# Macaron transformer block on 8 cores: four in-flight copy and square tiles instead of two in the layer-norm statistics of the attention stage

## What is computed

```python
def _layernorm(x, axis=-1, eps=1e-5):
    m = jnp.mean(x, axis=axis, keepdims=True)
    v = jnp.var(x, axis=axis, keepdims=True)
    return (x - m) / jnp.sqrt(v + eps)

# ffn: h = square(relu(x @ W_fc.T)); y = h @ W_proj.T;
#      five spiking steps on y, mean of the spikes (a sum of five thresholds)
# attn: layer norm, 16 query heads of 64 over one shared k and v, causal softmax, @ Wo
x = x + 0.5 * _L0_ffn_ref(_layernorm(x, axis=-1), W_fc, W_proj)
x = x + _L0_attn_ref(_layernorm(x, axis=-1), gamma, Wq, Wkv, Wo)
x = x + 0.5 * _L0_ffn_ref(_layernorm(x, axis=-1), W_fc, W_proj)
```

## Time and profile before

| what | us |
|---|---|
| the two runs | 2231.53 and 2278.68, median 2255.1 |
| the profiled execution | 2232.72 |
| span of its slowest core (core 4) | 2231.1 |
| spans of the other seven cores | 2206.0, 2221.2, 2229.1, 2223.8, 2226.0, 2227.9, 2219.5 |
| mean granted TensorE clock of core 4 | 0.792 |

### The profile page before, as it was taken

How to read it: one execution, slowest core, us unless ns; L and a number is a source line. 1 busy time by engine, 2 the same in 40 slices (tenths; PEclk the granted TensorE clock), 3 DMA queues, 4 the chain that set the end, 5 groups by cost and what they waited for, 6 DMA issues and landing times.

```text
span 2231.1 us, 21038 instructions; the slowest of 8 cores (2206.0 to 2231.1 us)
## 1 busy us (share of the span) xinstructions
PE 1468.6 (66%) x6244; PEld 574.1 (26%) x6244; DVE 777.2 (35%) x1498; ACT 618.9 (28%) x1644; POOL 91.1 (4%) x175
## 2 busy tenths in 40 slices
PE   0457759999973455535445454545395999999992
PEld 0023224444430111111111111111141344444441
DVE  0331047281623344442312211111134326454526
ACT  0311012120202000055565666666303202020200
POOL 1000100000022000000000000000100000000000
PEclk9979879999985698755555555555597899999996
DMA  9615921303045101034564667575832021323231
GB/s 212 128 47 148 211 76 35 127 22 130 20 111 85 35 14 23 12 57 85 111 124 87 128 114 132 100 128 112 140 119 86 10 108 68 119 79 118 78 112 57
DMA packets 319247, 206.73 MB, mean 93 GB/s; under 512 B 288778, under 2 KB 293002, under 8 KB 306850
## 3 DMA queue, kind: packets, MB, share of 16 engines
q1 hardware_dynamic: 293586, 104.28, 22.2%
q0 software_dynamic: 24400, 92.72, 16.0%
q10 hardware_dynamic: 1152, 8.39, 1.2%
HBM read 125.76 MB, written 25.25 MB: 68 GB/s over the span
## 4 chain that ended last, share of the span: by engine, by line
PE 50%; DMA 15%; DVE 14%; ACT 10%; issue 6%; another core or an unknown queue 3%; DVEq 1%; POOL 0%; ACTq 0%; SPq 0%; POOLq 0%
PE pb L447 18%; PE pb L393 14%; ACT WB L769 9%; DMA WB<-WB 8%; PE pb L663 5%; DVE acc L341 4%; PE pb L546 3%; PE pb L820 3%; DMA Q<-wprojT 2%; DMA Q<-X 2%; PE pb L235 1%; DMA R_t<-r_d 1%; ACT Q L399 1%; PE pb L685 1%
## 5 line engine op out<-in xcount | busy, mean ns | idle before, releaser
L393 PE MATMUL pb<-Q,WB 128*128 128x512 bf16 x2048 | 457.4, 384 | 75.8 <-DVE Q L369 49.8
L447 PE MATMUL pb<-HB,Q 128*128 128x512 bf16 x2048 | 450.6, 382 | 44.5 <-DMA Q<-wprojT 30.4
L769 ACT ACTIVATE WB<-pb,ncb 128x512 bf16<-128x512 f32 (+3 forms) x640 | 389.6, 644 | 240.8 <-PE pb L746 120.2
L399 ACT ACTIVATE Q<-pb 128x512 bf16<-128x512 f32 x256 | 152.9, 597 | 748.3 <-PE pb L393 663.5
L741 PE MATMUL pb<-WB,Q 64*128 64x512 bf16 (+3 forms) x320 | 151.2, 494 | 251.4 <-ACT WB L769 245.9
L393 PEld LDWEIGHTS pb<-Q,WB 128*128 128x128 bf16 x2048 | 199.2, 98 | 332.7 <-issue 104.9
L447 PEld LDWEIGHTS pb<-HB,Q 128*128 128x128 bf16 x2048 | 200.5, 98 | 294.6 <-issue 60.4
L402 DVE TENSOR_TENSOR HB<-Q 128x512 bf16<-128x512 bf16 x256 | 105.0, 424 | 191.9 <-ACT Q L399 185.2
L746 PE MATMUL pb<-WB,Q 64*128 64x512 bf16 (+3 forms) x320 | 156.8, 511 | 0.0
L663 PE MATMUL pb<-WB 128*64 128x512 bf16 x544 | 123.6, 629 | 42.7 <-DMA WB<-WB 42.6
L235 PE MATMUL pb<-Q,ones 128*1 128x512 bf16 x96 | 49.9, 520 | 151.0 <-DVE Q L225 92.2
(11 more groups left out here) (90 smaller groups left out, 801.4 us busy)
## 6 DMA issues: line engine op xcount, KB each, us to landing
Q<-wp POOLq DMA_DIRECT2D x56, 1024.0 KB, 5.1
X<-xin SPq DMA_DIRECT2D x8, 1024.0 KB, 38.6
WB<-wfcT POOLq DMA_DIRECT2D x8, 1024.0 KB, 47.9
Q<-wprojT POOLq DMA_DIRECT2D x32, 256.0 KB, 13.1
wp<-Q SPq DMA_DIRECT2D x8, 1024.0 KB, 8.8
wf<-WB ACTq DMA_DIRECT2D x8, 1024.0 KB, 19.7
WB<-wf POOLq DMA_DIRECT2D x8, 1024.0 KB, 19.7
xout<-X SPq DMA_DIRECT2D x32, 256.0 KB, 2.5
```

The lines of the kernel that those rows point to most:

```text
L393: P.emit("T", lambda E, par=par, dc=dc, fc=fc: E.matmul(PB[par][:], wfc_t(dc, fc), xn_t(dc)[:], start=(dc == 0), stop=(dc == DC - 1)), inc ...
L399: P.emit("A", lambda E, par=par: E.activation(hh_t(par)[:], PB[par][:], AF.Relu), inc=("a_rl", 1))
L447: st=st, sp=sp: E.matmul(PB[dc][:], wpe_t(par, fcl, dc), h_t(fc), start=st, stop=sp), inc=mark)
L769: b=(bA, bB)[hl], pc=pc, g=g, po=po: E.activation(p2_t(par, pc, hl, N), PB[b][:, 0:N], AF.Exp, bias=ncb[:, pc:pc + 1], scale=1.0, accum_ou ...
```

## The change

Only the gated variant of `ln_stats` changes, the one in `attention()`. The pair's tiles become four of each kind: `xb4(0..3)` in columns 12288 to 14335 of `Q3`, where both kinds were before, and `xq4(0..3)` in columns 14336 to 16383, which takes in the two tiles of `hh_t`. So one wait of ACT for the last square of the ffn (`v_h`) is added ahead of the loop. GpSimd's copy and ACT's square of pair k now wait for pair k-4. The copies signal on four semaphores, one for each tile, instead of two. The instructions themselves, their number, their sizes and their order on each engine are as before, and so is the variant of the two ffn stages, which stands below `continue` unchanged.

```diff
+        if sgate is not None:
+            P.wait("A", "v_h")
         for tb in range(NT):
             if xwait is not None:
                 P.wait("V", xwait[0], xwait[1](tb))
             for dc in range(DC):
-                par = dc % 2
                 k = tb * DC + dc
                 if sgate is not None:
-                    P.wait("G", "t_sx", max(0, P.val("t_sx") - 1))
+                    par = k % 4
+                    P.wait("G", "t_sx", max(0, P.val("t_sx") - 3))
                     P.wait("G", sgate[0], sgate[1](tb, dc))
                     P.emit("G", lambda E, dc=dc, tb=tb, par=par: E.dma_start(
-                        out=xb_t(par)[:], in_=xsl(dc, tb * 512)),
+                        out=xb4(par), in_=xsl(dc, tb * 512)),
                         inc=(f"g_xb{par}", 16))
...
+                    P.wait("A", "t_sx", max(0, P.val("t_sx") - 3))
+                    P.wait("A", sgate[0], sgate[1](tb, dc))
+                    P.emit("A", lambda E, par=par, dc=dc, tb=tb: E.activation(
+                        xq4(par), xsl(dc, tb * 512), AF.Square),
+                        inc=("a_sq", 1))
+                    P.wait("T", f"g_xb{par}")
+                    P.emit("T", lambda E, par=par, B0=B0, dc=dc: E.matmul(
+                        PB[B0][0:1, :], ones[:, 0:1], xb4(par),
+                        start=(dc == 0), stop=(dc == DC - 1)))
+                    P.wait("T", "a_sq")
+                    P.emit("T", lambda E, par=par, B1=B1, dc=dc: E.matmul(
+                        PB[B1][0:1, :], ones[:, 0:1], xq4(par),
+                        start=(dc == 0), stop=(dc == DC - 1)),
+                        inc=("t_sx", 1))
+                    continue
```

More of the change, by code:

```diff
@@ L210, in ln_stats, with xb4, xq4 @@
         P.wait("T", "v_on", 1)
+        def xb4(p):
+            return Q3[:, 12288 + p * 512: 12288 + p * 512 + 512]
+        def xq4(p):
+            return Q3[:, 14336 + p * 512: 14336 + p * 512 + 512]
+        if sgate is not None:
+            P.wait("A", "v_h")
         for tb in range(NT):
@@ L214, in ln_stats @@
             for dc in range(DC):
-                par = dc % 2
                 k = tb * DC + dc
                 if sgate is not None:
-                    P.wait("G", "t_sx", max(0, P.val("t_sx") - 1))
+                    par = k % 4
+                    P.wait("G", "t_sx", max(0, P.val("t_sx") - 3))
                     P.wait("G", sgate[0], sgate[1](tb, dc))
                     P.emit("G", lambda E, dc=dc, tb=tb, par=par: E.dma_start(
-                        out=xb_t(par)[:], in_=xsl(dc, tb * 512)),
+                        out=xb4(par), in_=xsl(dc, tb * 512)),
                         inc=(f"g_xb{par}", 16))
[L223 to L226, removed]
+                    P.wait("A", "t_sx", max(0, P.val("t_sx") - 3))
[13 more added lines that the diff above has]
+                    continue
+                par = dc % 2
+                P.wait("V", "t_sx", max(0, P.val("t_sx") - 1))
+                P.emit("V", lambda E, dc=dc, tb=tb, par=par: E.tensor_copy(
+                    xb_t(par)[:], xsl(dc, tb * 512)), inc=("v_xb", 1))
                 P.wait("A", "t_sx", max(0, P.val("t_sx") - 1))
@@ L229, in ln_stats @@
                     P.wait("A", xwait[0], xwait[1](tb))
-                if sgate is not None:
-                    P.wait("A", sgate[0], sgate[1](tb, dc))
                 P.emit("A", lambda E, par=par, dc=dc, tb=tb: E.activation(
                     xq_t(par)[:], xsl(dc, tb * 512), AF.Square), inc=("a_sq", 1))
-                P.wait("T", f"g_xb{par}" if sgate is not None else "v_xb")
+                P.wait("T", "v_xb")
                 P.emit("T", lambda E, par=par, dc=dc, B0=B0: E.matmul(
```

## The result

The changed kernel takes 2213.2 us in the median of 11 runs (2204.7 to 2236.6), the kernel before 2238.7 in the median of 10 taken beside it. The ratio is 0.9896, with a 95% interval of 0.9865 to 0.9927: 23 us less, or 1.0%. In some executions the cores of one half of the chip show a lower granted clock and the time is some per cent longer; the two medians count these, and all ratios and intervals leave them out. Forecast were 2207 us for the profiled execution and a gain of 25.6, which is a ratio of 0.9885.

A forecast was written before the change was run, and what follows sets the result against it. The attention statistics were taken as bound by copy latency, not throughput. Four buffers gave 24.4 us on core 4, plus 1.2 for the clock: 25.6 off 2232.7, so 2207 us; forecast's own range 2200 to 2213, full range 2197 to 2238.

The forecast's parts named there:

- What bounds the stage: Attention statistics: the copy's round trip, 4.05 us for two pairs in flight, sets the pace; no resource is full.
- A pair and a block: TensorE takes 0.85 us a pair; with four buffers pair 4 starts at 4.05 and the eight-pair block ends at 7.61.
- What is late next: Between blocks TensorE's wait for DVE to take both sums out comes into the open, 1.75 us.
- The delay by the spikes: First block: DVE's copies stand behind the last ffn block's spikes, so TensorE restarts at 692.2 instead of 689.6, costing 2.6 us.
- The sum: Core 4: 692.2, two blocks of 9.36 and one of 7.61; last matmul at 718.5 instead of 742.92, 24.4 us gained.
- The clock: TensorE at half clock, 0.50, in the stage; expected fast only at block ends, 1.2 us more gain.
- the rival in which TensorE runs fast throughout: TensorE at 2.4 GHz in the whole stage: 4.2 us more, gain 28.6, time 2204 us; chance 0.08.
- The part that I did count: Last pair of a block at fast clock takes 0.4 us less; three times 0.4 are 1.2 us.
- The rival that the copies slow one another: Each copy waits for three others on the DMA engines, loop 6.6 us, stage 49.8: gain 13 us, 2220; chance 0.08.
- a sign that I had named as one of being wrong: In the stage, copies that take over 2.6 us to land would show the forecast wrong.
- Core 4 stays the slowest: Other cores' spans are 2 us and more shorter, so core 4 was taken to stay the slowest.
- Behind the stage: Copies, square roots, attention and f2 move forward as a whole; time coming back there would show the forecast wrong.

The follow-up runs named there:

- e_bank_block1: The changed kernel with only the second block's sums moved to PSUM banks 2 and 3: stage 35.3 us, time 0.9865 of the kernel before.
- e_banks4: Against the changed kernel: eight tiles of each kind, a PSUM bank pair for each block, two places for the sums; 0.9767 and, rerun, 0.9805 of the kernel before.

## Why the prediction was right, point by point

**What bounds the stage.** Right, and shown from both sides: two tiles for the copies alone give back the whole 63 us, four of them alone give the whole gain, and three lie between.

**A pair and a block.** The terms of the block came out within a few hundredths of a microsecond up to the fifth pair: 0.85 a pair (0.80 to 0.86), pair 4 at 4.05 (4.10 on core 3). The block ended at 7.44 instead of 7.61: the faster clock at its end gave 0.41, and the eighth pair started 0.24 later than forecast, at 6.84.

**What is late next.** The pause of 1.75 us is there, as 1.86: DVE starts 0.17 behind TensorE as forecast, and TensorE 0.25 behind DVE, where I had taken 0.15 from another line. The delay by the spikes is there too; DVE starts 0.30 us behind the last spike and not 0.1. On core 4 the pause was forecast as 4.4 us. The trace has

```profile
689.78 0.58 PE L237 MATMUL pb<-Q,ones 128*1 128x512 bf16 x1 [4.41 <-DVE stg L269]
```

and `e_bank_block1` shows that this wait is a cost, 3.3 us net in the median of the cores.

**The sum.** On core 4 the stage was forecast as 37.1 us (718.5 - 1.2 - 680.22) and is 38.6, 676.84 to 715.45; before it was 62.7. Of the 1.5 us, 0.7 come from the first matmul, which stood 10.96 us ahead of the end of the spikes instead of 10.29, 0.3 from the slower restart behind them, and 0.5 from the three blocks and two pauses that follow. Over the cores the stage fell from 63.2 to 38.6 in the median, 24.6 us, where I had 25.6.

The forecast held the point behind this, that the second block waits for the spikes. So on every core the stage ends 27.3 to 28.3 us behind the last spike, and a core whose first matmul comes early only waits longer: the stage is 36.1 us on core 3, which starts 8.5 us ahead of the end of its spikes, and 41 us on cores 1, 5 and 7, which start 12.5 to 13 ahead.

That the profiled execution came within 2 us of the forecast, 2208.9 against 2207, is in part luck. Core 4's span fell by 30.1 us: 24.1 from the stage, 3.4 because the stage began earlier, and 2.6 behind it. On core 3, now the slowest, the stage gave 27.1 and the part behind it 2.4, but it began 12.9 us later than before, so its span fell by 16.5. The 2230 that I gave for a median over runs that spread like the two shown was 17 us too high: the runs of both kernels spread less.

**The clock.** The direction was right, the reasoning on what a fast clock throughout would give was wrong in one step. I had a block at 2.4 GHz end at 6.2 us, with the last three copies following the first at 0.64. Core 4 had a block whose first five pairs were all at 2.4 GHz:

```profile
708.29 0.38 PE L237 MATMUL pb<-Q,ones 128*1 128x512 bf16 x1 [1.86 <-DVE stg L269]
...
711.88 0.38 PE L237 MATMUL pb<-Q,ones 128*1 128x512 bf16 x1 [1.70 <-DMA Q<-X]
...
712.79 0.42 PE L237 MATMUL pb<-Q,ones 128*1 128x512 bf16 x1 [0.32 <-DMA Q<-X]
...
713.58 0.58 PE L237 MATMUL pb<-Q,ones 128*1 128x512 bf16 x1
```

The fifth pair starts at 3.59, where 3.64 was forecast, but the next two pairs come 0.91 and 0.79 apart, the clock falls back to 1.2 GHz among them, and the block takes 7.16 us in all, hardly less than the 7.44 of core 3 whose first five pairs were slow. The shortest of the 32 blocks, on core 0, took 6.94. The 0.64 came from the rate of large weight loads; the copies' own pace with a full queue, which `e_banks4` shows, is near 0.77. GpSimd issued the last four copies 0.58 apart (four in 2.31 us), so the wider spacing arose between issue and landing. So the clock went from 0.50 to 0.77, and the rival in which TensorE runs fast throughout would have been worth less than its 4.2 us: no block came near the 6.2 us that it needs. The part that I did count, 0.4 us for each of the last three blocks, came out as 0.1, 0.3 and 0.5 on core 4.

The Trainium skill, "TensorE: Matmul & The Clock Gate" (part 1), says that the throttled clock is the default and that activity releases it. The trace agrees in the second block of core 4: behind a pause of 4.41 us the matmuls of its first three pairs, which follow one another without idle time, take 0.58 to 0.63 us, and from the end of the fourth pair on they take 0.38. What that was worth had to be read from the copies.

**The rival that the copies slow one another** has its part of truth. The median from issue to landing goes from 2.3 us to 2.4 with four tiles, 3.3 with eight and 3.9 without pauses. With four the median hides a sign that I had named as one of being wrong, copies that take over 2.6 us: in the first block the slowest copy was used 2.9 to 4.6 us after its issue on seven of the eight cores (3.77 on core 4). Their cause stays open; two such copies, of 4.1 and 4.2 us, stand on core 7 of the kernel before too. They lengthen the first block, to 8.5 us on core 4, and cost nothing, since the second block waits for the spikes anyway.

**Core 4 stays the slowest.** Wrong for this execution, and it could not have been forecast from one trace. The first matmul of the stage was on core 3 at 671.40 before and at 684.34 after, on core 4 at 680.22 and 676.84. These starts come out of f1, where nothing was changed, and differ by up to 13 us on one core from one execution to the other. The last spike ends at 675 to 691 us over the cores before, and 682 to 693 after. A stage's own length agrees between cores within 5 us; the time of the slowest core takes in this scatter.

**Behind the stage** all moved as a whole: 17.3 us to the attention before and 17.2 after, and 1465 to 1470 to the end of the span in every kernel. On some cores the load of the means (`MU_t`) now comes late, with a wait of 2.06 us on core 3, 1.46 on core 0 and 0.70 on core 6, where it was at most 0.53 before:

```profile
738.44 6.17 DVE L536 TENSOR_TENSOR HB<-X,MU_t 128x512 bf16<-128x512 f32 x8 [2.06 <-DMA MU_t<-mu_d]
```

## What to carry to other kernels

Where a loop waits for a DMA whose engines are at less than half, divide the round trip (issue, landing, use, release) by the number of buffers, and deepen until that is below the next limit; deepen only the operand whose round trip it is. Before counting the gain, ask what the wait had hidden: here it was the copy-out of the sums at each block's end and, for the first block, an unrelated queue of DVE work ahead of that copy-out, 8 us of 39 on core 4, and another pair of accumulators removes it. Read such a change by its own stage over all cores, measured from the event that holds it (here the last spike); the time of the slowest core has a scatter of several microseconds that comes from elsewhere, and the mean of all the cores' spans has less.

## What the runs showed of the hardware that I had not expected

- A copy of 128x512 from f32 to bf16 within SBUF, issued by GpSimd, lands every 0.77 us with the queue full, in a stretch where the engines moved 179 GB/s at a DMA share of 1.19. The share of 0.42 with two in flight had given 0.84, and the weight loads' 207 GB/s had given 0.63: the pace lies between.
- Issues of GpSimd whose waits are met go at 0.55 us each (seven in 3.84 us, in `e_banks4`). With waits that have only just been met they stand 0.85 apart in the changed kernel, at the pace of the pairs that release them.
- TensorE went to 2.4 GHz and back within the stage at different points on different cores, for the same program: the mean granted clock of the stage is 0.71 to 0.81 over the cores with four tiles, 0.52 to 0.64 with three, and 0.50 on all cores with two.
